# Gated delta-rule layer with MLP on one Trainium2 core: every operation of the pair loop gets its own distance behind the newest pair, and the first transpose of the inverse becomes a masked product on GpSimd

## The reference

```
xn  = layernorm(x)
q, k, v = split(silu(causal_conv4(xn @ Wqkv)));  z = xn @ Wz
beta = sigmoid(xn @ Wb);  g = -exp(A_log) * softplus(xn @ Wa + dt_bias)
q, k = l2norm(q) * 128**-0.5, l2norm(k)
for t:                       # per sequence and head, state M is 128 x 128
    M = M * exp(g_t);  M = M + outer(k_t, (v_t - k_t M) * beta_t);  o_t = q_t M
o   = o * rsqrt(mean(o*o) + eps) * norm_w * silu(z)
x   = x + layernorm(o @ Wout)
x   = x + layernorm(relu(relu(layernorm(x) @ W1' + b1) @ W2' + b2) @ W3' + b3)
```

## Time and profile before

| | us |
|---|---|
| median of 3 runs | 3135.22 (3133.44 to 3136.01) |
| the profiled execution's own time | 3138.29 |
| its span | 3136.5 |

### The profile page before, as it was taken

One profiled execution on the slowest core, in us unless ns is written; L12 is line 12 of the kernel. 1 busy time (PEld: TensorE's weight loads), 2 busy tenths in 40 slices (PEclk: granted clock), 3 DMA queues, 4 the chain that ended last, 5 costly groups with the idle time before them and its releaser, 6 DMA issues. The chain is left out here.

```text
span 3136.5 us, 69866 instructions
## 1 busy us (share of the span) xinstructions
PE 2815.4 (90%) x24116; PEld 2299.9 (73%) x24116; DVE 2405.6 (77%) x5534; ACT 2050.9 (65%) x6902; POOL 1363.4 (43%) x1522
## 2 busy tenths in 40 slices
PE   3499999999999999999999999999999999986998
PEld 2377777777777777777877787777778777773544
DVE  5588888888888888888888888888888888863443
ACT  1477777777777777777777777777777777761221
POOL 2245454445444544545454545445454545440010
PEclk8799999999999999999999999999999999996999
DMA  5322222222223222222222222222222222211010
GB/s 175 136 79 89 82 72 78 88 72 78 82 62 92 78 88 78 74 81 88 67 83 82 82 71 71 97 62 88 82 86 67 85 82 75 75 42 42 28 39 27
DMA packets 78994, 243.54 MB, mean 78 GB/s; under 512 B 8384, under 2 KB 21568, under 8 KB 61888
## 3 DMA queue, kind: packets, MB, share of 16 engines
q1 hardware_dynamic: 78656, 239.18, 24.2%
HBM read 225.52 MB, written 13.63 MB: 76 GB/s over the span
## 5 line engine op out<-in xcount | busy, mean ns | idle before, releaser
L771 DVE SCALAR_TENSOR_TENSOR conv<-pj,taps_now,conv 128x511 f32<-128x511 f32 (+2 forms) x1152 | 855.7, 743 | 48.4 <-ACT conv L644 38.9
L965 PE MATMUL pj<-xt,w_hi 128*128 128x512 f32 x2048 | 688.6, 417 | 25.3 <-DVE wo L759 23.4
L601 POOL TENSOR_TENSOR oc<-oms,halves 128x4 f32<-128x4 f32 x128 | 130.2, 1017 | 955.6 <-DVE oms L884 955.6
L579 POOL TENSOR_TENSOR kq<-kq,cum 128x512 f32<-128x512 f32 x256 | 323.7, 1285 | 285.4 <-issue 269.0
L965 PEld LDWEIGHTS pj<-xt,w_hi 128*128 128x128 f32 x2048 | 350.5, 191 | 80.9 <-DVE wo L759 23.8
L965 PE MATMUL pj<-xt,w_lo 128*128 128x512 f32 x1024 | 407.5, 398 | 0.0
L644 ACT ACTIVATE conv<-pj,taps_now 128x512 f32<-128x512 f32 x384 | 264.7, 689 | 193.6 <-PE pj L965 193.6
L701 ACT ACTIVATE x<-bk 128x256 f16<-128x256 f32 x512 | 197.3, 385 | 205.5 <-PE bk L1052 205.3
L1118 PE MATMUL pj<-wo,yt 128*128 128x256 f32 x1024 | 284.8, 401 | 13.8 <-DVE yt L892 1.1
L663 ACT ACTIVATE squares_out<-tr 128x128 bf16<-128x128 f32 x1024 | 270.1, 294 | 0.3 <-PE tr L972 0.3
L636 ACT ACTIVATE u<-st,f 128x128 f32<-128x128 f32 x512 | 187.8, 367 | 119.9 <-PE st L1079 90.5
(11 more groups left out here) (163 smaller groups left out, 7461.5 us busy)
## 6 DMA issues: line engine op xcount, KB each, us to landing
xt<-xt_scratch SPq DMA_DIRECT2D x129, 1024.0 KB, 7.1
decay<-decay_scratch SPq DMA_DIRECT2D x129, 256.0 KB, 4.9
cum<-cumdecay_scratch SPq DMA_DIRECT2D x128, 256.0 KB, 3.3
w_raw<-in_w_heads SPq DMA_DIRECT2D x17, 512.0 KB, 3.3
xt_scratch<-xt_hi SPq DMA_DIRECT2D x8, 512.0 KB, 2.8
xt_scratch<-xt_lo SPq DMA_DIRECT2D x8, 512.0 KB, 3.8
res<-in_x SPq DMA_DIRECT2D x8, 512.0 KB, 4.6
out<-yo SPq DMA_DIRECT2D x8, 512.0 KB, 3.1
```

Source lines behind the costliest of these rows:

```text
L579: last = nc.gpsimd.tensor_tensor(part, part, s.of(cum, 1)[:, :], ALU.mult)
L771: nc.vector.scalar_tensor_tensor(out=conv[:, i, j:SEQ], in0=pj[:, i % 2, 0:SEQ - j], scalar=taps_now[:, i, TAPS - 1 - j:TAPS - j], in1=con ...
L965: last = nc.tensor.matmul(pj[:, i % 2, :], w[:, kt, cols], x_[:, kt, :], start=(n == 0), stop=(n == 3 * KT - 1))
```

## The change

It has these parts.

- `Step` and `steps` go. Each operation takes a pair number p; every engine runs one loop over a from 0 to 131 (`PAIRS + LAST_STAGE`), and each call in it has its own distance, `a`, `a - 1` to `a - 4`. `real(p)` leaves out what lies outside the 128 pairs.
- The lists are in another order on all engines. An operation may be in another step than its stage had it: `turn_o`, `gated`, `out_sums`, `out_norm`, `out_project`, `add` and `out_squares` are at a-4 (were at a-3), `grams`, `decay_b` and `decay_qk` at a (were a-1), `z_level`, `mask_level` and `tx_level` of level 3 at a-1 (were a-2), `solve(0)`, `state_update(0)`, `from_state_k(1)`, `rhs(0)`, `rhs(1)`, `state(0)` at a-2 (were a-3), `gates`, `k_norm` and `q_norm` at a-1 (were at a).
- `x_first` and `take_first` go, and with them the semaphore `tx_done[0]`. `first_transpose` on GpSimd makes x16 as b_hi times a mask, the transpose of the level 0 mask, which is appended to the mask table. It is the same matrix, since t16 is the transposed b_hi under that mask.
- `split` comes in the last slot of a head for Q and K, and in the first slot of the next head for V and Z. Each waits for the projection that last used the weights.
- The taps are read from `cw` itself; `taps_now` and its copy go. GpSimd's spare instructions ahead of the splits and of `unit_diagonal` go.
- More waits are written out (on buffers that had been safe by the old order), such as `mask_first` on `res_done`, `decays` on `b_raw` and `qk_ready`.
- SyncE issues per step xt, decays, cumulated decays and, at a head's first slot, the weights, in this order.

The diff, cut to its core:

```diff
@@ tables and helpers
+LAST_STAGE = 4
+    masks.append(masks[0].T)
+    def wait(eng, s, count):
+        if count > 0:
+            eng.wait_ge(s, min(count, PAIRS))
...
@@ SyncE
+    for a in range(PAIRS):
+        if a + 1 < PAIRS:
+            wait(sp, proj[Z], a)
+            load_xt(a + 1)
+            wait(sp, e_ready, a)
+            load_decay(a + 1)
+        wait(sp, m_ready[CH - 2], a - 3)
+        sp.dma_start(of(cum, a)[:, :], row(cumdecay_dram, a)).then_inc(of(cum_in, a), DMA)
+        if a % NSEQ == 0 and a // NSEQ + 1 < HEADS:
+            sp.wait_ge(w_split, 4 * (a // NSEQ) + 4)
+            sp.dma_start(w_raw[:, :, :], w_heads[a // NSEQ + 1]).then_inc(w_in, DMA)
@@ GpSimd
+    def split(i, head):
+        if head < HEADS:
+            cols = slice(P * i, P * i + P)
+            pool.wait_ge(w_in, DMA * (head + 1))
+            wait(pool, proj[i], NSEQ * head)
+            nc.gpsimd.tensor_copy(w_hi[:, :, cols], w_raw[:, :, cols]).then_inc(w_copied[i], 1)
+            pool.wait_ge(w_copied[i], head + 1)
+            nc.gpsimd.tensor_tensor(w_lo[:, :, cols], w_raw[:, :, cols], w_hi[:, :, cols].bitcast(F32),
+                                    ALU.subtract).then_inc(w_split, 1)
...
+    def first_transpose(p):
+        if real(p):
+            wait(pool, b_hi_ready, p + 1)
+            wait(pool, inv_ready, p - 1)
+            nc.gpsimd.tensor_tensor(of(x16, p)[:, :, :], of(b_hi, p)[:, :, :],
+                                    mask[:, P + (LEVELS - 1) * HALF:].unsqueeze(1).to_broadcast([P, CH, P]),
+                                    ALU.mult).then_inc(tx_ready[0], 1)
...
+    for a in range(PAIRS + LAST_STAGE):
+        head, slot = a // NSEQ, a % NSEQ
+        scale_b(a - 1)
+        if slot == 0 and head:
+            split(V, head)
+        unit_diagonal(a - 1)
+        out_norm(a - 4)
+        if slot == NSEQ - 1:
+            split(Q, head + 1)
+        scale_kq(a - 1)
+        first_transpose(a - 1)
+        if slot == 0 and head:
+            split(Z, head)
+        low_b(a - 1)
+        if slot == NSEQ - 1:
+            split(K, head + 1)
+        scale_k_tok(a - 1)
+        k_norm(a - 1)
+        inverse(a - 2)
@@ ScalarE
+    for a in range(PAIRS + LAST_STAGE):
+        take(3, a - 2)
+        out_squares(a - 4)
+        state_input(1, a - 3)
+        high_b(a - 1)
+        gates(a - 1)
+        take(4, a - 2)
+        convolve(Q, a)
+        take(5, a - 2)
+        state_input(2, a - 3)
+        convolve(K, a)
+        take(1, a - 1)
+        activate(Q, a)
+        take(6, a - 2)
+        convolve(V, a)
+        squares(turned_q, 1, sums_q, a)
+        activate(K, a)
+        state_input(3, a - 3)
+        take(2, a - 1)
+        correction(a - 2)
+        squares(turned_k, 0, sums_k, a)
+        activate(V, a)
+        take_k(a)
+        state_input(0, a - 2)
+        take_out(a - 3)
+        take_v(a)
@@ VectorE
+    for a in range(PAIRS + LAST_STAGE):
+        gated(a - 4)
+        out_sums(a - 4)
+        mask_level(4, a - 2)
+        state(1, a - 3)
+        add(0, a - 4)
+        mask_first(a - 1)
+        rhs(2, a - 3)
+        mask_level(5, a - 2)
+        add(1, a - 4)
+        mask_level(1, a - 1)
+        q_norm(a - 1)
+        rhs(0, a - 2)
+        convolve(Q, 1, a)
+        convolve(Q, 2, a)
+        mask_level(6, a - 2)
+        convolve(Q, 3, a)
+        convolve(K, 1, a)
+        mask_level(2, a - 1)
+        state(2, a - 3)
+        convolve(K, 2, a)
+        rhs(3, a - 3)
+        convolve(K, 3, a)
+        convolve(V, 1, a)
+        residual(a - 2)
+        convolve(V, 2, a)
+        convolve(V, 3, a)
+        decays(a)
+        norms(a)
+        mask_level(3, a - 1)
+        inverse_norm(a)
+        decay_b(a)
+        state_scale(a)
+        state(0, a - 2)
+        decay_qk(a)
+        rhs(1, a - 2)
@@ TensorE
+    for a in range(PAIRS + LAST_STAGE):
+        turn_o(a - 4)
+        solve(1, a - 3)
+        z_level(4, a - 2)
+        out_project(0, a - 4)
+        state_update(1, a - 3)
+        tx_level(4, a - 2)
+        z_first(a - 1)
+        out_project(1, a - 4)
+        from_state_k(2, a - 3)
+        z_level(5, a - 2)
+        project(Q, a)
+        z_level(1, a - 1)
+        tx_level(5, a - 2)
+        solve(2, a - 3)
+        project(K, a)
+        z_level(6, a - 2)
+        tx_level(1, a - 1)
+        out_bank_free(a - 3)
+        outputs(0, a - 3)
+        state_update(2, a - 3)
+        outputs(2, a - 3)
+        outputs(1, a - 3)
+        tx_level(6, a - 2)
+        z_level(2, a - 1)
+        project(V, a)
+        from_state_k(3, a - 3)
+        turn_q(a)
+        tx_level(2, a - 1)
+        residual(a - 2)
+        solve(3, a - 3)
+        project(Z, a)
+        correction(a - 2)
+        turn_k(a)
+        grams(a)
+        z_level(3, a - 1)
+        solve(0, a - 2)
+        outputs(3, a - 3, signal=o_done)
+        turn_v(a)
+        state_update(0, a - 2)
+        tx_level(3, a - 1)
+        from_state_k(1, a - 2)
```

More of the change, by code:

```diff
@@ L418, in delta_heads, with real, of @@
     added = [sem(f"added{i}") for i in range(2)]
[L420 to L458, removed]
+    def wait(eng, s, count):
+        if count > 0:
+            eng.wait_ge(s, min(count, PAIRS))
+    def real(p):
+        return 0 <= p < PAIRS
+    def of(bufs, p):
+        return bufs[p % len(bufs)]
     def chunk(c):
@@ L496, in _ @@
                 sp.dma_start(ident4[:, c, :], identity).then_inc(consts_in, DMA)
[L497 to L520, removed]
+            load_decay(0)
+            for a in range(PAIRS):
[9 more added lines that the diff above has]
+                    sp.dma_start(w_raw[:, :, :], w_heads[a // NSEQ + 1]).then_inc(w_in, DMA)
         @block.gpsimd
@@ L526, in _ @@
             pool.wait_ge(filled, 2)
[L528 to L536, removed]
@@ L622, in _ @@
-            steps(pool, run)
+            def split(i, head):
[7 more added lines that the diff above has]
+                                            ALU.subtract).then_inc(w_split, 1)
@@ new lines, in z_first, with z_level @@
+            def z_first(p):
+                if real(p):
+                    wait(pe, b_hi_ready, p + 1)
+                    wait(pe, qk_ready, p + 1)
+                    for c in range(CH):
+                        last = nc.tensor.matmul(g0[:, chunk(c)], of(b_hi, p)[:, c, :], ident16[:, :], start=True, stop=True)
+                    last.then_inc(z_done[0], 1)
+            def z_level(level, p):
+                if real(p):
+                    ps = g0 if level < 3 else bk
+                    wait(pe, y_ready[0] if level == 1 else tx_ready[level - 1], p + 1)
+                    if level == 3:
+                        wait(pe, inv_raw, p)
+                    for c in range(CH):
+                        last = nc.tensor.matmul(packed_of(ps, c, level), of(b_hi, p)[:, c, :],
+                                                half_of(of(t16, p), c, level, 0), start=True, stop=True)
+                    last.then_inc(z_done[level], 1)
@@ new lines, in tx_level @@
+            def tx_level(level, p):
+                if real(p):
+                    ps = g1 if level < 3 else bk
+                    wait(pe, y_ready[level], p + 1)
+                    if level == 1:
+                        wait(pe, tx_ready[0], p + 1)
+                    for c in range(CH):
+                        last = nc.tensor.matmul(packed_of(ps, c, level), of(x16, p)[:, c, :],
+                                                half_of(y[level], c, level, 0), start=True, stop=True)
+                    for c in range(CH):
+                        last = nc.tensor.matmul(packed_of(ps, c, level, 1), y[level][:, c, :],
+                                                half_of(of(x16, p), c, level, 1), start=True, stop=True)
+                    last.then_inc(tx_done[level], 1)
@@ new lines, in residual @@
+            def residual(p):
+                if real(p):
+                    wait(pe, tx_ready[LEVELS - 1], p + 1)
+                    wait(pe, b_lo_ready, p + 1)
+                    for c in range(CH):
+                        nc.tensor.matmul(bk[:, chunk(c)], of(b_hi, p)[:, c, :], of(t16, p)[:, c, :], start=True, stop=False)
+                        last = nc.tensor.matmul(bk[:, chunk(c)], of(b_lo, p)[:, c, :], of(t16, p)[:, c, :], start=False, stop=True)
+                    last.then_inc(res_done, 1)
@@ new lines, in correction, with solve @@
+            def correction(p):
+                if real(p):
+                    wait(pe, res_ready, p + 1)
+                    for c in range(CH):
+                        last = nc.tensor.matmul(bk[:, chunk(c)], yr[:, c, :], of(x16, p)[:, c, :], start=True, stop=True)
+                    last.then_inc(fix_done, 1)
+            def solve(c, p):
+                if real(p):
+                    if c == 0:
+                        wait(pe, inv_ready, p + 1)
+                        wait(pe, u_ready[CH - 1], p)
+                        wait(pe, m_ready[CH - 2], p)
```

(2 more changed lines are left out.)

904 lines of the change are left out of this document (354 added, 550 removed).

## The result

| | us |
|---|---|
| before, median of 4 runs | 3135.6 (3133.4 to 3139.1) |
| after, median of 4 runs | 3169.9 (3167.6 to 3171.7) |
| ratio | 1.0108, 95% interval 1.009 to 1.0125 |
| profiled execution after: own time, span | 3171.7, 3169.7 |

The change made the kernel 34 us slower. The forecast was 3060; the slower rival had said 3154.

What follows compares the result with a forecast made beforehand. TensorE was taken to bound the kernel. Work 18.55 + waits 0.38 + 0.62 + 0.72 + edge 0.18 = 20.45 us a pair against 21.09: 82 us less, +5 for the ends, said as 3060 us; 8-in-10 range 2985 to 3170.

Steps and rivals of the forecast that it cites:

- the slower rival: Before solve(0): the scan holds inverse, TensorE idles 0.75 us more a step, 3154 us; chance 0.30, milder form included.
- the scan and `inverse` at 0 us: Before solve(0): VectorE's decays scan and GpSimd's inverse don't block each other, 0 us in the sum.
- the head's edge: Last slot of a head: split(Q) delays x16, project(V) 2.15 us late, up to 0.7 regained; 1.45 us a head.
- the ends of the loop: Filling and emptying the loop: one step more but the same chain, 0 to +10 us, taken as +5.
- (a): End of the step: TensorE idles 0.38 us as from_state_k(1) needs m[0] from the state step.
- (b): Start of the step: TensorE idles 0.62 us between turn_o and out_project(0), on the path through VectorE's gated.
- (c): Middle of the step: GpSimd holds q_norm and rhs(0), convolutions come late, TensorE idles 0.72 us ahead of project(V).
- The sum: Whole kernel: step 20.27 us plus 0.18 for the edge, 20.45 against 21.09 us a pair, 82 us less.

Runs made afterwards that it cites:

- Run 1: Kernel after with one call moved on VectorE: the decays scan ahead of convolve(V, 2) instead of behind convolve(V, 3); 3103.8 us.
- run 4: Kernel after with, in a head's last slot, GpSimd's split(Q) moved behind first_transpose and split(K) behind k_norm; 3097.1 us.
- Runs 6 and 10: 6: kernel after, first transpose back on TensorE, its copy on ScalarE, 3031.6 us; 10: the same with q_norm and rhs(0) behind convolve(Q, 3), 3040.2 us.
- run 2: Kernel after with q_norm and rhs(0) moved behind convolve(Q, 3) in VectorE's list; 3064.2 us.

## Why the prediction was wrong

**The failed step: the scan and `inverse` at 0 us.** The sum took no cost for their meeting, "since the rows nearest in kind of engine work (convolutions beside `inv`) show none". They are not the nearest in what counts. A convolution reads one input from PSUM and passes; the scan reads both from SBUF, and it doesn't. `inverse` took 2.12 us, and TensorE idled 0.76 us ahead of `solve(0)`, where the rival had 0.75. Run 1 shows that it is this meeting: without it `inverse` takes 1.16 us and the kernel 66 us less. The rival's step of 21.02 us was measured as 21.06. Its total, 3154, was 16 us short: the head's edge cost more than it had, and the ends of the loop less. The section "Who interferes with whom" of the Trainium skill's "SBUF — State Buffer", which I had cited for it, says that a VectorE instruction with two SBUF inputs contends with a GpSimd instruction that reads SBUF, and by the rows of after and of run 1 that is so for this pair. No run varied where the inputs lie, so that the inputs are the reason is the page's statement and not shown here. I had a rule for this very pair of instructions and put my weight on rows of another kind.

The trace of before has one meeting of the scan with a GpSimd instruction after all, in the first two steps:

```profile
136.72 1.02 POOL L594 TENSOR_TENSOR kn<-k,halves 128x4 f32<-128x4 f32 x1 [1.58 <-DVE k L788]
...
136.76 1.22 DVE L780 TENSOR_TENSOR_SCAN e<-decay,ident 128x512 f32<-128x512 f32 x1
```

The scan isn't held by this one: it takes 1.22 us, where its median is 1.19. So a GpSimd instruction on 128x4 values passed beside the scan, and one on 128x512 did not. Which of the two `inverse` would be like couldn't be read from it.

**The head's edge: the wait as walked, the clock behind it missing.** Predicted 1.45 us a head, 2.15 lost in the last step and 0.7 won back in the next. Measured 2.9: the last step takes 25.04 us and the next 20.05, beside 21.07, so 3.97 lost and 1.02 won back. The queue behind `split(Q)` was as walked (the product ended at 1112.31, 3.0 us after TensorE was ready for it; I had 2.8), and without the 1.9 us that the low clock costs an edge (see run 4, an estimate) the last step loses 2.1, as said. I had the clock at nothing.

**(a), (b) and (c) held.** End of step 0.31 against 0.38, start 0.57 against 0.62, middle some 1.0 against 0.72, in the kernel as it is, with the product in it; `r[0]` rose above 1 us and the convolutions were late, as walked. The middle was somewhat dearer since `tx_level(6)`, whose mask stands behind the convolutions, also waited, which the walk had not looked at. `turn_o` has no wait on `o`.

**The sum, mended.** 20.45 + 0.80 (step: 21.07 against 20.27) + 0.19 (edge: 2.9 us a head, so 0.37 a pair, against 0.18) = 21.44. That is 0.99 x 128 = 127 us on 3060, or 3187. The rest, 17 us, is in the ends, to within 3 us: behind the last pair's scan the kernel before needs 348 us (3136.5 - 2788.3) and the kernel after 336 (3169.7 - 2833.7), and the first scan is 3 us earlier, where I had put +5.

**What the prediction saw and did not count.** It had the product in GpSimd's unbroken run as one of five items, and (c) as the price of the order. Runs 6 and 10 show that (c) is the price of the product in that place: the same order without it has no (c), and no wait at the head's edge. I never priced the two parts of the change apart, so a product of 1.16 us on an engine with "some 10 us of work in a pair" looked free. Apart, the order is a gain of 103 us and the product a loss of 138 in it.

## What to carry to other kernels

When two engines lock each other out, a busy share says little: ask for each instruction that can hold or be held (here a scan with both inputs in SBUF and a tiny `tensor_scalar`) what the other engine is doing at the moment when it comes, and who is queued behind it. Price the parts of a change apart and in each other's company, since a product of 1.16 us changed the time by -12, +138 and -31 us in three orders, the last two of which differ by a few lines. And where a new wait of the matmul engine is long (3 us here), look at the granted clock behind it, and at more than one such place, before putting it down at its length.

## What the hardware showed that I had not expected

- One meeting holds both engines in turn: the scan (1.22 us) held GpSimd's `inverse` (1.16 became 2.12), and that held a VectorE instruction on 128x8 values for 1.06 us instead of 0.16. In 126 of 128 steps the scan started 0.04 to 0.12 us ahead, and `inverse` took over 2.0 us.
- A wait of 3 us can cost TensorE more than its length. In the kernel after the granted clock fell to 0.50, the 1.2 GHz level, at all fifteen edges (0.50 from 1113 to 1118 us), in a loop that otherwise shows 1.00; in run 2, with the same wait of 2.9 us, at seven of fifteen. Where it fell, the step was 1.6 or 2.7 us longer than where it did not (24.7 or 25.8 us against 23.1). The waits of 0.5 to 0.8 us in each step did not lower it.
